# Another order of turns on the five engines, and other PSUM banks, in a two-layer network of four mixers on one core

## What is computed

```python
x = L0_attn_x                                   # (8, 256, 128)
xn = _layernorm(x)
x = x + gated_linear_attention(xn) + local_transformer(xn)    # L0_attn, L0_ffn
xn = _layernorm(x)
x = x + delta_rule(xn) + moe_attention(xn)                    # L1_attn, L1_ffn
```

```python
xv = einsum('bsd,hedp->bshep', x, v_w); v = einsum('bshep,bshe->bhsp', xv, gate_v)
att = softmax(einsum('bhqp,bhkp->bhqk', q, k) * SCALE); ctx = einsum('bhqk,bhkp->bqhp', att, v)
out = einsum('bshep,hepd->bsd', ctx[:, :, :, None, :] * gate_o[..., None], o_w)
```

## Time and profile before

| | us |
|---|---|
| median of 3 runs | 1290.52 |
| the profiled execution, its own time | 1297.51 |
| its span, first to last instruction | 1295.0 |
| PE busy (matmuls) | 1175.6 |
| VectorE (DVE) busy | 971.2 |
| GpSimd (POOL) busy | 851.1 |
| ScalarE (ACT) busy | 721.9 |

### The profile page before, as it was taken

The page is one execution under the profiler, slowest core; times in us unless marked ns, Lnnn a source line. Parts: engine busy times, 40 slices in busy tenths (PEclk is TensorE's granted clock), DMA queues, the critical chain, the costliest instruction groups (busy, mean ns, idle before and its releaser), DMA issues.

```text
span 1295.0 us, 31167 instructions
## 1 busy us (share of the span) xinstructions
PE 1175.6 (91%) x11890; PEld 930.8 (72%) x11890; DVE 971.2 (75%) x1950; ACT 721.9 (56%) x2060; POOL 851.1 (66%) x1157
## 2 busy tenths in 40 slices
PE   5778799899999798899999999989999898989898
PEld 3455477777678677777778777877688776878686
DVE  5858799876995969877687977968768956865354
ACT  5787876458655562567456665437666533332322
POOL 3746466686787727787568754887639876865841
PEclk9999989999999999999999999999999999999999
DMA  6111165555376438764566563775348565767673
GB/s 255 34 38 34 37 237 191 167 192 163 100 242 207 139 105 264 233 200 130 178 205 210 153 193 124 265 243 171 101 135 262 185 220 183 268 223 250 222 249 125
DMA packets 91186, 230.87 MB, mean 178 GB/s; under 512 B 9888, under 2 KB 16160, under 8 KB 90912
## 3 DMA queue, kind: packets, MB, share of 16 engines
q1 hardware_dynamic: 90896, 228.30, 54.3%
q10 hardware_dynamic: 144, 0.59, 0.1%
HBM read 225.71 MB, written 3.15 MB: 177 GB/s over the span
## 4 chain that ended last, share of the span: by engine, by line
PE 32%; DVE 24%; ACT 5%; DMA 4%; issue 3%; POOL 0%; DVEq 0%; ACTq 0%; POOLq 0%
PE bank L899 8%; PE bank L946 6%; DVE ogate L1352 5%; PE bank L827 3%; PE bank L936 2%; DVE dy L1210 2%; DVE kv L1123 2%; DMA kv<-values 2%; PE bank L612 2%; PE bank L917 1%; PE bank L927 1%; DVE mmin L1341 1%; PE bank L647 1%; DMA ogate<-gates 1%; PE bank L671 1%
## 5 line engine op out<-in xcount | busy, mean ns | idle before, releaser
L1748 POOL TENSOR_TENSOR vgate<-vgate,xT 128x512 f32<-128x512 f32 x256 | 330.3, 1313 | 102.4 <-DMA vgate<-gates 102.1
L899 PE MATMUL bank<-wv,vgate 128*128 128x128 f32 x2048 | 257.5, 280 | 6.4 <-DVE prob L1055 2.4
L899 PEld LDWEIGHTS bank<-wv,vgate 128*128 128x128 f32 x2048 | 245.3, 194 | 17.4 <-issue 5.2
L946 PE MATMUL bank<-ogate,wo 128*128 128x256 f32 x1024 | 244.4, 385 | 7.7 <-DVE ogate L1352 6.7
L946 PEld LDWEIGHTS bank<-ogate,wo 128*128 128x128 f32 x1024 | 189.8, 191 | 40.6 <-issue 14.3
L1352 DVE TENSOR_TENSOR ogate<-ogate,bank 128x1024 f32<-128x1024 f32 x128 | 152.9, 1212 | 33.3 <-PE bank L936 30.3
L1463 ACT ACTIVATE prob<-prob,mx 128x128 f32<-128x128 f32 (+1 forms) x256 | 96.0, 377 | 53.7 <-DVE mx L1059 53.4
L1681 POOL TENSOR_TENSOR rot<-rot 128x512 f32<-128x512 f32 x64 | 81.6, 1275 | 56.6 <-DVE rot L1035 56.2
L1630 ACT ACTIVATE mprob<-bank,mmin 128x256 f32<-128x256 f32 x128 | 59.2, 468 | 104.3 <-DVE mmin L1341 104.1
L1724 POOL TENSOR_TENSOR step<-dlt,uw 128x126 f32<-128x126 f32 (+22 forms) x248 | 92.5, 373 | 24.7 <-DVE dlt L1275 8.7
L1726 POOL TENSOR_TENSOR dlt<-dlt,step 128x126 f32<-128x126 f32 (+22 forms) x248 | 95.4, 385 | 19.4
(11 more groups left out here) (227 smaller groups left out, 2493.1 us busy)
## 6 DMA issues: line engine op xcount, KB each, us to landing
vgate<-gates SPq DMA_DIRECT2D x128, 512.0 KB, 4.5
ogate<-gates SPq DMA_DIRECT2D x128, 512.0 KB, 4.2
wv<-in_wv_moe SPq DMA_DIRECT2D x128, 256.0 KB, 4.8
wo<-in_wo_moe SPq DMA_DIRECT2D x128, 256.0 KB, 4.6
kv<-values SPq DMA_DIRECT2D x64, 256.0 KB, 4.5
local<-in_local SPq DMA_DIRECT2D x1, 1715.0 KB, 10.6
wqkv<-in_wqkv SPq DMA_DIRECT2D x2, 768.0 KB, 7.0
x<-in_x SPq DMA_DIRECT2D x8, 128.0 KB, 5.3
```

Of the source, the lines that this page charges most:

```text
L899: i = nc.tensor.matmul(out[:, n * D:(n + 1) * D], xg[:, e, n * P:(n + 1) * P], m.wv[slot][:, e, :], start=(q, n, e) == (0, 0, 0), stop=(q, ...
L946: i = nc.tensor.matmul(out[:, 0:T], m.wo[slot][:, e, :], cg[:, e, :], start=(h, q, e) == (0, 0, 0), stop=(h, q, e) == (MH - 1, 1, EQ - 1))
L1748: i = tt(gate[:, e:e + half, :], gate[:, e:e + half, :], spread(m.xT[b % 2][:, :], 1, half), ALU.mult)
```

## The change

The five strings of turns and the string of banks are replaced. They were drawn under the rule that VectorE's operations between SBUF tensors and GpSimd's operations exclude each other in time. The rest of the file stays as it was: the same stages, the same instructions, shapes and transfers, as many letters in each string. A line of each string stands for the others:

```diff
 TENSOR_TURNS = (
-    "GaaaaGGGaaaaabbXababbbbaGbababbabacaaacabGGbcacabGGcbbbaaabGbbaabbaaabbbGGaGcbGabcbbbcbcbGcbbGabaacaacGaaacbbc"
+    "GaaaaGGGaaaaaXbbaabbbGbabbaabaGbbabacaaacbGbaGGcacbbcbbbGaaabbGGbGbaabGaaabbcabacbbbcbGcbbGcbbaaabGcaaGGcaaabc"
...
 VECTOR_TURNS = (
-    "VaaaaaaaGaabaabbaGGGbGbaGGbbGGbaaGGaaGGcacabcaabbGGGGbccccbGbaabGaabaabaabbGcGcGbbcGbGbGGbGGGccccGGaaGGcaaGcGG"
+    "VaaaaaaaGaaaaabGGbbGGbbaGbGGbGaabGGaaGGGGaacGGcaabcbbGbbccccbbGaabGaaaabGaacbbGGGcbGcbGGbbGGbGGcccGGcGGGaaGaac"
...
 BANK_TURNS = (
-    "76543210765204375643275037265403726507365270632532072536017253617205365204136750124507351243601243560124356012"
+    "76543210765204375627507462357046357064503675403617034536174074536105734621734260753026430742653704267503467503"
```

More of the change, by code:

```diff
@@ L88 @@
[L88 to L92, removed]
@@ new lines @@
+    "bDADDGaaaDAbbaDDbGcaAAVcDaVAcGVbVbDDPcEbPbbPAbGcbPzbAPAPAPaGVAaaAAaAPPaaCVAGVAAaaFCAaVaVPVAPAAaVAVbGGPAbbGAPDD"
+    "FFbDPcDADDCcDGADDFcDPcDDAVcDADDzAVDADDVPDbVDDAbCADAVDDbAbDbCbVbGbbAGDDPPEbAAPAbVbPcAPAVcAaPAcacaaPcAVAACVAaaaa"
+    "abPAVAAaPbaVbaAabbaPbbVbaAaPabAAbbAVbGFcPDADPcVDGcAcDVGADPcDADVDDaADVADDabAPDbGDDaVDADDaVDGDDAPDbDDAAFADGGGFVa"
+    "DVPFEAaDaVVaaVbbbbVaaabbabPVGAAGbAbacbPcaAPPcGbbVAAacGGAacGazPAbbAGPCAbaPCAbbbaGPaaFGbaGaCAbAAbVcAVVcDDVAacPcA"
+    "APDcADbFDDbFDFADDPDPAVAVADDbzGPDbADDbAAVADVDDbbDGADDCbDbDDCbPDbPbAAVADVDcAPcCPEPAAVAVcGFAcPGAAVAcaGPAaaaPPAAGF"
@@ L95 @@
+    "APaaPFAaaaVbbDAADVAaVbDaVAaaaVDbDbbGPaAAVAaaVabAaDDbbPaDDPaAADbAbDDPDbADDcDbbDDVDcVDDbDbbDDcbbPDcAAVbbAPDDcAGb"
+    "bVFGbacaaGPcPAEAVAVcaPAcAVAcAVzaaAaPPaCACVAVAbaPbaAPPAAVFAVbCbPAbbbAAVbAVbVbbAPbDDVPVAADGAVDcADDGFFFDPPVDDcVAG"
+    "PDAPDDcAVDGDDGDADDVDADDADGADDVVDcAGPDDcVzVPVAAPAEPPACAACAPFAAAPACPDDVVAPDAAVAVVDPDDAPAAVADVDDPDADDPDADDADFDDAP"
+    "DPDDADFDDAADFAPVDDAPAAVAVPAPAEAVAPPAAAVAPPAVAAVAPPAVAAVAPVAPDDAAVDADPDDVDADPDDADDAVDADDPDVDDADPDDADADDAPDPAADP"
     "PE")
 VECTOR_TURNS = (
-    "VaaaaaaaGaabaabbaGGGbGbaGGbbGGbaaGGaaGGcacabcaabbGGGGbccccbGbaabGaabaabaabbGcGcGbbcGbGbGGbGGGccccGGaaGGcaaGcGG"
@@ new lines @@
+    "caacbaaabbGbGcccGcabzCbbaaCbaaGCCCCCaaCAaaaCCAbaFcbbFcaacFaabbVVFGGbGccOOcGGGcAFzCAFCVaaVbGaOOaAbFFAGGVVFbGGcb"
+    "GbcGOOcbCCCCCbCVCVACbAbDDVbVGDOOcccGGAcAVVOOAAFOcaaVVcAcaaAFOFVVGFccccaOOaAFbAGaabbDFFOObFDADFGADDDGDbDGGDaaDb"
+    "VDVGaaDOObGDbVVGDGADAGaaDGGGaaDcGGGGcDcDAVVGDbAGVbbDDVbcEccDObOacbbzaObCOCAAGaaOOaaAAVVaaGOOaaAFAVCVCFCAVCVOAC"
+    "FOCCDFCODODFFVVGcDDcDcDAFDFAGFGGcccDGGGcDGzDCODCDAVVODAbGGDbbDVVOODbAbDAbDVbDVCCCDDbCECDAOAOCCaCcaOOcVVGcGAGaa"
+    "AGcccGGGaacGOOVAVAaabaabOObVVbaaAbaaAbbbDaaOOAVVAFcFcDcDFOODFcccVVDGcADADaaDVVODbODbbDGDbADAVDVGDDDOODADFFDAGa"
@@ new lines @@
+    "aVVGGGEFFaaDDFbaabbDaaabGGGGGVVOOAGAGcabcGGcbGGGbGbVVOOaacccAGAczCGaaCVVbOObGCCCCaabCCACCAbaaFDFAcFAVVcOcDOFGG"
+    "GVVcccODOAcDbADGFDFGDbbDFFbOFOGGAVDzCAVGCDbDObOGADGVADVGDbDGDGDbGCCCCDCDCDOCCAOAVVDDGcGGcDEcOOAVAVFFcccaOaAOAc"
+    "FGaaFaaOOAGFADaaFaaVVbOObbDAbAVVDaaVVDaaDbGObOAaAaVVbaaDbDODAOADDDcDbDbbDcVDbVcDbDbbDbDOOccDAcADDcVVFFFaacDaac"
+    "GEOOAcGAVVGGGGGGcccOOGAcAVzCVaaCaaOCCOACAVVCCbCbbCCAbOAOVVbFbbOOAbDAVVFFDOVVDAOADFcGDGGGFDFFFGFGDcVVOcODGGDADA"
+    "DDDGDVDVODOADAGDDDcccGDDcDzCCVVOOAEAVVOCCACACCCCOVVCOADAOFDFDAVVODAOFDVVODAFDAODDDVDODODAFVADDDFDODFDADAFOFDDV"
@@ new lines @@
+    "VDOAOAVVOEOVAVAOOAAVVOOAAVVOOAADVVDOODADADVDVDDODODADADVDDDODODAADDDOOE")
+SCALAR_TURNS = (
+    "GaaaaaGGGaaaaGaaaaabaXababbbbaabbbaabbaabaaacaacaabcaaGbcbGbabbGabbbaabGGbaaaaabGaabGaaacbacbcbbbbcbbbababaaac"
+    "aaacaGaacbGaaabGcaababCabbbGaaGGCaCAaaaabbGFaabAbaaabaaAbCAacbacbaacFaabcAFbbFACAaFaAaaabbAbaAbAbFbbAcCbcCacab"
+    "AabbbAAbCbAbcAbbAaAbAAAAFAAacacaAaaAGcGFcAaaFGAFaaAaAbaaAabFADDbFAGAGGAaaGbaababAaabbabAaAaAbababaacaAacDcDAbA"
+    "bEcbAbbbabbACAAaGAaGAaaaAaAaCAaGAaaaFCAaaaAAAaAbAGAFbbGFDDFbFcACcGAcAGFcAACAAbACAbbAbDbbDACAbbbEbAbAAbaAcAacca"
+    "AcaAaAaaACaAaaAaabAaaAaaabbaaaAbbbaAbabAaaabAabbAbAFDAcDccFcGAGFAAaAaaAbGabAaAaAbAFGDGADGaGAFaEAaFaaaabbbaaabb"
+    "baaabAbbAaaAcbcaAcbbAacGGAaAGaCAaabCAbbaCaGaabbbAGbFaGACAabaAbaAcDADcFcAaFGcAAFAbFAbFAAbCAAbAbAAbAbCbbCbbDDbAA"
+    "AAcECcAAcAFAcAaAaAGAaGFaaFAaaGFAaAaAaaaFaaDbADbAaAbaaAaaaaaabAbbaaAAaaAbbaabaaAbbAAbAcbbcbcbbbbDcADbbAAAabGbGb"
+    "FaacaGEacAaGAAcaAcAAAaCAaaaCaCAaAaAaAbAbFACAbAbbbAbbAbAbbAbDDFAAAFAcFFFcAcAAGAGAGAADDcACAEAAACACAFAAACAADDAAAA"
+    "AAFAFAAAFAAAFADDAAFAAAAAEAAAAAAAAAAAAAAAADDAAAAAAAAAAADDAE")
@@ new lines @@
+GPSIMD_TURNS = (
+    "aaaaaaaabGGbbGGabaGaaGGaaGaabbbGabaaaaaabaGbGGbGbGGGaaGaaaaababGbaabaaaaaabaWWWbaaaGWWWGGbaWaabaGWWGGbbWWbDWGW"
+    "bDGDDWWWDWDDaaaWaWaDaDaaGbbDDDDDDGWDDaDaaDabWGDDbGWDaDGaGaaDWGGWWGbWDbWDDDDDDaaaaWDaWaWaaDWWbbGDDDDDDWGWDGDWDG"
+    "DWDWDWGDbDWDbWbWDbDDDWDWaGaDaaWDaaaabWDbaaGabaDbWaGaGWWWDWDDWDDaDWaDWDbDGDbDWDDDWDaaGWWaWaDabaWaGbGGaDDGWGbDGG"
+    "bDaWaGDaabDWDaaDbWaaWWWWGDDDDGDbDbGWDWDDbGDDWDGDDWDbGWDGGWDDDDDDDaaaDaWaaaWaWbWbGDWWaaaDaDWbWaWaaDabWDDDDDDDbD"
+    "DbDWDWbbWDaWDDaDaWaWDWaaWaaDWWDbDbWDbWGbGGWGWWWDWDDWGGDGDWDWGDDDDDWDDDWDGWWDDDDDDDDDWWWWWDWDWWDDDWDDWDDDDDDDDD"
+    "WDDWWDWDDWDWDWDWWWDDWDDDDDDDDDDDDD")
@@ L130 @@
 SYNC_TURNS = (
[L131 to L134, removed]
+    "xxxGGGGGGGGGGGGGGGGGGGGGGGCvvvooovvvoovGGovvGGoovvovvCoovvvvooovvooooGGGGvGvvvGGGGvvvvoEoxooooovoovvvvooGoGGGG"
@@ L137 @@
+    "ooCvvvovvvovvvGGGGooEoxvoovoovCvovovovovoovvovvovvoGGGGGvvoEvxvvvovGGGGooovoooGoGGGGCvvvvoooovvGGovvGGoovvoCoo"
+    "EvvxovooooovvvvvovvooovvovoGvGGGGooEvvovvoovvooovvCovvvovovGGvGGoovvoovvvvovvovoEooooCovvovvvoovvooooovovvooEv"
+    "oovoovvoovvovovoooooE")
 BANK_TURNS = (
-    "76543210765204375643275037265403726507365270632532072536017253617205365204136750124507351243601243560124356012"
-    "35610523651075162073516253105341367247035707641506473647156034715647031657046576340753475145034715030475430743"
@@ new lines @@
+    "64756104370517054173605241706532410537620342421047634763214076032607134126203467207162371623746213746721467124"
+    "67124614276214761427614261276444612756142571625716721421675214675217462175174365127436125741326714726472624212"
+    "41712641264172614624624412461443136436514360531464532146532164536246354261542375413754213764135643526426465427"
+    "16524152615642156425652656124612464124156416457142576542075405702750745270452720534052743504325732457302430572"
+    "03542304250423750423507425070425340724374230423407234072147023147021370415207146205714271047210214702626062062"
@@ new lines @@
+    "02602603250632506353075243604357260440574263657460746374537367507364507643576403530306435406530453045430345030"
+    "45030450345703504735017251402751402751074517045017465017654027610762540712650746175021704650172650426154021542"
+    "60154620154062510642516405217526475026470521670562356107325607320573627053203672656503752375276305276370532760"
+    "32760365067507600767267264726727726706706207352075320540124512651265124572164524135465617176416742674216742617"
+    "463172635721430275613205673105276130526735021753017231075213025")
```

43 lines of the change are left out of this document (2 added, 41 removed).

## The result

| | us |
|---|---|
| median of 4 runs | 1248.87 (1244.05 to 1249.26) |
| the kernel before beside it, 4 runs | 1291.07 (1286.07 to 1293.31) |
| ratio | 0.967, 95% interval 0.9633 to 0.9707 |
| the profiled execution, its own time, its span | 1249.26, 1246.9 |

What follows compares the result with a forecast made beforehand. PE was taken as nearly full, with many short waits, partly for VectorE instructions held up by GpSimd. Terms -15 - 5 + 5 + 0 + 0 = -15 us took 1290.5 to 1275.5 us; range 1252 to 1304.

Steps and rivals of the forecast that it cites:

- the exclusion: VectorE instructions reading two SBUF tensors wait for the end of GpSimd's instruction; on top comes about one L1748, 1.30 us.
- The collision term: Order of VectorE and GpSimd: fewer collisions, between nothing and all 49.9 us, taken as -15 us.
- the sum over four lines: VectorE's busy time beyond count times shortest duration for L1210, L1296, L1207 and L1168: 49.9 us together.
- My own test: Four-line sum falls from 49.9 to below 30 us if collisions went; if it stays and kernel is faster, PE's cover.
- More cover in the loops of batches 4 and 6: More PE work inside these chunk loops, 11.8 us in batch 4, cuts PE's waits for L1296 and L1352: -5 us.
- The last loop: Batch 7's chunk loop keeps 23.3 us of PE work after losing 18.5; PE loses what it lasts beyond: +5 us.
- Rival 3: Slower: last chunk loop becomes the kernel's end, PE stands 11.7 us, 1302 us; decides from 3.3 us a chunk; chance 0.22.
- Banks and loads: Redrawn PSUM bank lists, -2.4 to +2.4 us, and SyncE's load order, DMA 4% of the chain: each taken as 0.
- Rival 1: Order does not do what it says: collisions stay near 50 us and fall elsewhere, 1290 us; chance 0.20.
- Rival 2: VectorE comes first nearly everywhere, GpSimd waits, all 49.9 us of VectorE go: 1262 us; chance 0.10.

## Why the prediction was right or wrong

**What bounds it, and the exclusion: right.** PE's list with short waits, and VectorE's two-SBUF-input instructions waiting for GpSimd. Taking GpSimd's reads away shortened L1210 to 485 ns everywhere.

**The collision term, -15 us: this is the step that failed, in its form and in its size.** I wrote "With that share the 49.9 us cost the kernel 16 us", and took 15 us of that as gained because collisions go. Neither half held. Their price was 67 us for the 108 us of them (the sum over four lines left out half), 0.62 for each and not 0.32. The share was too low for two reasons. It came from a chain that was followed for 68% of the span only: where it was followed, 317 of VectorE's 654 us lie on it, 0.49. And it took an average over all of VectorE's time, where a collision is not average time: of the collisions in that stretch 58.5 of 80.6 us lie on the chain, 0.73. Counted so in the new kernel it is 0.08, and the price measured there is 8 for 98, also 0.08; this way of counting, on one trace each and on the part that could be followed, came nearer to both measured prices than mine. Why a collision is worse than average is my reading and was not tried by itself: everything behind it on VectorE is late by it, and PE's list has no other work there. It is not one price either: 20 us for 27 in the choice, 16 for 26 in the convolution, nothing that shows for 17 in the chunk loop. And what the new order brought down is the price of a collision, from 67 us for 108 to 8 for 98, not their number. My own test said so beforehand: "if it stays and the kernel is faster, PE's cover did it".

**More cover in the loops of batches 4 and 6, -5 us: right in kind, and part of the larger thing.** The two waits went from 4.8 and 6.7 us to 0.3 and 2.8, 8.4 us of the 11.5 that could go. The loop of batch 4 lasts 47.5 us now, where it took 35.0, and that of batch 6 32.6, where it took 24.6, as they hold more of PE's work. I had counted this cover in two places and priced it by the waits that PE has at these two lines. The rest was elsewhere: the convolution's collisions cost 16 us in the old order and nothing that shows in the new one, and PE's wait for L1637 on ScalarE, which I gave nothing, fell by 6.8 us. What each loop's cover brought by itself was not measured.

**The last loop, +5 us: over-sized, as far as its length tells.** It took 1232.07 - 1206.32 = 25.75 us, 3.7 a chunk, for 23.3 us of work on PE: 2.5 us. Rival 3 had its point at 3.3 a chunk, and it was passed by little.

**Banks and loads, 0:** nothing in the waits contradicts it. That the new order is 17 us slower where no collision happens stood nowhere in my sum; it was within what I had left to rival 3 as "what a redrawn list loses".

**The rivals.** Rival 1 (collisions stay, time stays) had the first half right, and its argument, that the lists do not say when two engines run, fits the excess; the sentence I set against it, that such an order leaves time behind the waits, was the one to build the forecast on. Rival 2 (VectorE comes first) is out: L1748 still makes VectorE wait, and its own mean went only from 1313 to 1322 ns. Rival 3 (slower by the last loop) is out with the loop's 25.75 us.

**The range.** Its lower end was rival 2 with 10 us more. The upper bound that I had written down, all 49.9 us, would have reached 1241; I did not let it into the range, as I held the chain's share for a measurement.

## What to carry to other kernels

A stall's price is not its length times its engine's share of the chain: it depends on what the waiting list has to do meanwhile, and ran here from nothing to some three quarters of the length. Before a chain's share is used as a factor, add the shares up; what they lack of 100% was never followed. Then ask how much of the stalls themselves lies on the chain, not how much of the engine. This order of turns did not keep two engines apart that exclude each other (98 us of collisions where there were 108), but it left little waiting behind the meetings; without the exclusion it was 17 us the slower, so such an order is worth drawing again when the instructions change.

## What the runs showed of the hardware that I had not expected

GpSimd's writes alone do not stretch VectorE's instructions with two SBUF inputs: L1296 lasts 224 to 227 ns in all 64 cases beside the memsets that are all of GpSimd's 777 us. A tensor_scalar from SBUF to SBUF, which has one input, is still stretched beside memsets now and then (the second row), while a reduction with one SBUF input never did beside the original instructions (398 to 421 ns in 96 cases):

```profile
L1296 DVE TENSOR_TENSOR dlt<-dlt,gates x64: 224/224/227, 304.7 to 1201.8; 128x64 f32<-128x64 f32 x64
```

```profile
L1207 DVE TENSOR_SCALAR dy<-pad,layer x24: 344/353/691, 159.5 to 1055.9; 128x256 f32<-128x256 f32 x24
```

The page "SBUF — State Buffer" of the Trainium skill, section "Who interferes with whom", separates the same three cases: an instruction with two SBUF inputs contends with a GpSimd instruction that reads SBUF and not with one that only writes it; one in a mode that uses two ports for one input, which tensor_scalar can enter, contends with GpSimd without that distinction; and a reduction never contends. The trace agrees for the first and the third (224 to 227 ns, 398 to 421 ns). For the second it shows the stretching (up to 691 ns), but not the mode.
